# A causal attention layer and a two-layer shifted transformer on one core: stages joined early, whole rows copied one partition down, results stored from ScalarE's queue

## The reference

```
xn  = layernorm(x)
out = x + attn(xn) + ffn(xn)
# attn: 16 heads of 64, causal, relative position bias per head (a table over i-j), logits / 64,
#       softmax, @ v, heads joined @ Wo + bo
# ffn:  two layers, each
h = shift_token(x)                 # columns 64..127 come from the token before
q, k, v = split(h @ wqkv)          # 8 heads of 64
q = l2norm(q) * q_scale; k = l2norm(k) * k_scale; q, k = rotary_xpos(q, k)
x = x + local_attention(q, k, v) @ wo      # windows of 64, looking one window back
h = layernorm(shift_token(x)) * ln_g + ln_b
a, g = split(h @ w1 + b1)          # 341 columns each
x = x + (a * gelu(g)) @ w2 + b2
```

## Time and profile before

| | |
|---|---|
| time, 3 runs | 2707.05 us median (2701.14 to 6372.38) |
| profiled execution | 2707.02 us, its span 2705.2 us |
| TensorE matmul busy | 2547.8 us (94%), 24208 instructions |
| ScalarE / VectorE / GpSimd busy | 2158.3 (80%) / 2009.4 (74%) / 1629.7 us (60%) |
| mean granted TensorE clock | 0.977 of full speed |
| DMA packets | 128513, 77.07 MB |

### The profile page before, as it was taken

How to read it: one execution, slowest core, us unless ns; L and a number is a source line. 1 busy time by engine, 2 the same in 40 slices (tenths; PEclk the granted TensorE clock), 3 DMA queues, 4 the chain that set the end, 5 groups by cost and what they waited for, 6 DMA issues and landing times. The chain is left out here.

```text
span 2705.2 us, 71234 instructions
## 1 busy us (share of the span) xinstructions
PE 2547.8 (94%) x24208; PEld 1988.1 (73%) x24208; DVE 2009.4 (74%) x5647; ACT 2158.3 (80%) x6335; POOL 1629.7 (60%) x1947
## 2 busy tenths in 40 slices
PE   7999999999999999999599999997979999999796
PEld 4777777777777777777378888885767888888575
DVE  4666666666666666666389999995659999999565
ACT  5888888888888888888389999996438999999642
POOL 3444444444444444444389999994229999999521
PEclk8999999999999999999799999998989999999898
DMA  2000000000000000000311111111111111111112
GB/s 72 7 7 10 9 9 5 8 7 9 9 9 5 10 7 7 9 6 5 103 41 41 38 42 39 38 42 46 33 26 40 38 42 42 38 40 42 46 33 79
DMA packets 128513, 77.07 MB, mean 28 GB/s; under 512 B 80196, under 2 KB 110736, under 8 KB 128144
## 3 DMA queue, kind: packets, MB, share of 16 engines
q1 hardware_dynamic: 127968, 72.34, 10.9%
q10 hardware_dynamic: 176, 0.07, 0.0%
HBM read 17.58 MB, written 8.41 MB: 10 GB/s over the span
## 5 line engine op out<-in xcount | busy, mean ns | idle before, releaser
L306 POOL TENSOR_SCALAR L<-L,rinv 128x128 f32<-128x128 f32 (+3 forms) x1024 | 522.4, 533 | 622.7 <-DVE rinv L488 622.7
L370 ACT ACTIVATE L<-L,nmax 128x384 f32<-128x384 f32 (+3 forms) x1024 | 571.8, 561 | 144.2 <-DVE nmax L474 144.2
L474 DVE CUSTOM_DVE_ANT_0 L<-bank,bias_tab 128x256 f32<-128x256 f32 (+3 forms) x1024 | 470.5, 479 | 180.3 <-PE bank L590 178.3
L886 ACT ACTIVATE f_L<-bank,f_nmax,f_rn 128x128 f32<-128x128 f32 x1024 | 459.9, 486 | 5.0 <-DVE f_nmax L1013 5.0
L863 POOL TENSOR_TENSOR f_rn<-f_ssq,f_mhalf 128x16 f32<-128x16 f32 x128 | 419.1, 3274 | 18.2 <-DVE f_ssq L997 4.7
L845 POOL TENSOR_TENSOR f_qkr<-f_ab 128x256 f32<-128x256 f32 x512 | 414.3, 838 | 10.3 <-DVE f_ab L964 10.3
L611 PE MATMUL bank<-ident,L 128*128 128x128 f32 x2560 | 370.4, 276 | 2.3 <-DVE PT L215 2.0
L611 PEld LDWEIGHTS bank<-ident,L 128*128 128x128 f32 x2560 | 296.8, 141 | 83.4 <-issue 46.1
L964 DVE TENSOR_TENSOR f_ab<-bank,f_tab 128x512 f32<-128x512 f32 x512 | 347.8, 680 | 8.8 <-ACT f_sq L876 8.8
L632 PE MATMUL bank<-PT,v 128*64 128x512 f32 (+3 forms) x2048 | 303.9, 439 | 0.6 <-DVE yacc L507 0.4
L632 PEld LDWEIGHTS bank<-PT,v 128*64 128x64 f32 x2048 | 126.8, 136 | 166.2 <-issue 164.9
(11 more groups left out here) (145 smaller groups left out, 6390.8 us busy)
## 6 DMA issues: line engine op xcount, KB each, us to landing
f_vm<-f_v SPq DMA_DIRECT2D x224, 128.0 KB, 2.4
f_hs<-xf SPq DMA_DIRECT2D x132, 32.0 KB
f_hs<-xf SPq DMA_DIRECT2D x132, 31.8 KB
xb<-in_L_attn_x SPq DMA_DIRECT2D x16, 256.0 KB, 2.8
out<-yacc SPq DMA_DIRECT2D x32, 128.0 KB, 1.8
f_hs<-xf SPq DMA_DIRECT2D x32, 128.0 KB
out<-f_acc SPq DMA_DIRECT2D x4, 1024.0 KB, 7.5
f_hs<-xf SPq DMA_DIRECT2D x32, 127.0 KB
```

The source lines that it names most:

```text
L306: nc.gpsimd.tensor_scalar(t, t, rinv[:, h % RING, a, i:i + 1], 1.0, ALU.mult, ALU.mult).then_inc(s_N, 1)
L370: nc.scalar.activation(t, t, ACT.Exp, bias=nmax[:, ep % RING, a, i:i + 1], scale=-1.0, accum_out=rsum[:, ep % RING, a, i:i + 1]).then_inc( ...
L474: nc.vector.tensor_tensor_reduce(out=L[:, p % RING, a, LOFF[i]:LOFF[i] + (i + 1) * P], in0=ps_s[a][i], in1=bias_tab[:, 2 * p + a, T - (i + ...
L886: nc.scalar.activation(L[:, ot % 2, a, k, :], ps_s[a][:, k * P:k * P + P], ACT.Exp, bias=nmax[:, ot % 2, a, k:k + 1], scale=rn[:, ot % 2, ...
```

## The change

- **Layers unrolled.** The loop over the two layers is written out; addresses are constants.
- **Block between removed.** Its loads and masks go into the causal stage: GpSimd builds the masks in slot (0, 6), SP loads the first shifted tiles in batch 1 and layer 0's tables and weights in batch 15 into the bias table's space, GpSimd multiplies the tables and splits `wqkv` in the last three slots (`prepare_attention`, eight steps).
- **Attention to MLP.** Batch 0's statistics to low half, batch 1's statistics and the halves of `w1` go into attention's drain slots. The MLP's loads of batches 0 and 1 go into attention's batches 4 and 5.
- **MLP to attention.** Layer 0's MLP loads layer 1's tables and weights in slots 4 to 6, its first shifted tiles in slots 7 to 10, and prepares them on GpSimd in slots 7 to 14.
- **MLP rows.** Four buffers; batches 0 and 1 are copied as before, the others as below; ScalarE writes the unshifted half.
- **MLP order.** `hidden(0)`, `hidden(1)`, transposes, `second` in one run, `hidden(2)`; VectorE's second gating comes before the residual.
- **End.** `out` is read back in tile (6, 0) of layer 0's attention. In layer 1's MLP GpSimd adds `xf` to `acc` batch by batch, VectorE adds the product to `acc`, and ScalarE's queue stores each batch.
- **Causal slot 4.** On ScalarE `value_out` and `xT_high` stand before an exponential each, on VectorE `xT_low` before the addition to `yacc`.

The core of the diff:

```
@@ causal_attention, sync
+                if b == B - 1:
+                    sp.wait_ge(s_L, at(b, 8 * HP, 8 * 4))
+                    for part in range(3):
+                        load_attention_weights(sp, c, d, w, 0, part, w["s_load"])
+                if b == 1:
+                    sp.wait_ge(s_xf, 1)
+                    sp.wait_ge(w["s_hs_zero"], 1)
+                    for t in range(TT):
+                        load_shifted(sp, c["hs"], xf, 0, t, w["attn"][f"hs{t}"])
@@ causal_attention, gpsimd
+                if (b, p) == (0, 6):
+                    build_masks(nc, pool, c, w)
+                for n in {(B - 1, 6): (0, 1, 2), (B - 1, 7): (3, 4, 5), (B, 0): (6, 7)}.get((b, p), ()):
...
+                    prepare_attention(nc, pool, c, w, n, w["s_load"])
@@ causal_attention, scalar
+                if p == 4 and item is not None:
+                    value_out(item)
                 exps(2, 1)
-                if item is not None:
+                if p == 4 and has_scores(b) and has_next(b):
+                    xT_high(b + 1, 1 - par)
+                if p != 4 and item is not None:
                     value_out(item)
                 exps(0, 1)
@@ causal_attention, vector
                 logits(3, 0)
+                if p == 4 and has_scores(b) and has_next(b):
+                    xT_low(b + 1, 1 - par)
                 if step is not None:
@@ load_shifted_batch
-def load_shifted_batch(sp, hs, xf, b, r, s_hs):
+def load_shifted_batch(sp, w, xf, b):
+    hs, s_hs = w["shifted"][b % 4], w["mlp"][f"hs{b % 4}"]
+    if b < 2:
+        sp.dma_start(hs[:, :, 0:half], x_b[:, :, 0:half]).then_inc(s_hs, 16)
+        sp.dma_start(hs[1:P, :, half:D], x_b[0:P - 1, :, half:D]).then_inc(s_hs, 16)
+    else:
+        sp.dma_start(hs[1:P, :, :], x_b[0:P - 1, :, :]).then_inc(s_hs, 16)
+    sp.dma_start(hs[0:1, 1:TT, half:D], x_b[P - 1:P, 0:TT - 1, half:D]).then_inc(s_hs, 16)
+def batch_own_half(nc, act, w, xf, b):
+    act.wait_ge(w["mlp"][f"hs{b % 4}"], batch_rows_count(b))
+    nc.scalar.activation(w["shifted"][b % 4][:, :, 0:half], xf[:, b * TT:b * TT + TT, 0:half],
+                         ACT.Copy).then_inc(w["mlp"]["half"], 1)
@@ local_attention
+            if b in (4, 5) and t == 0:                                    # sync
+                sp.wait_ge(w["s_fill"], 4)
+                sp.wait_ge(sem["x_out"], 2 * TT)
+                load_shifted_batch(sp, w, xf, b - 4)
+            if (l, b, t) == (0, 6, 0):
+                sp.dma_start(w["acc"][:], d["out"].rearrange("b (t p) d -> p (b t) d", p=P)).then_inc(w["s_acc"], 16)
+            if (b, t) == (B, 1):                                          # gpsimd
+                batch_scale(nc, pool, w, 0)
+            if (b, t) == (B, 2):
...
+            if (b, t) == (B + 1, 0):
+                batch_low(nc, pool, w, 0)
+            if (b, t) == (B + 1, 0):                                      # scalar
+                batch_affine(nc, act, c, w, 0)
+            if (b, t) == (B, 0):                                          # vector
+                batch_statistics(nc, dve, w, 0)
+            if (b, t) == (B, 2):
+                batch_normalise(nc, dve, w, 0)
+                batch_statistics(nc, dve, w, 1)
+            if (b, t) == (B, 3):                                          # tensor
+                batch_transposes(nc, pe, c, w, 0)
@@ gated_mlp
-        load_attention_weights(sp, c, d, 1 - l, sem["weights"])
-            sp.wait_ge(sem["hn"], at(b, TT, -TT))
+            if 2 <= b < B:                                                # sync
+                sp.wait_ge(sem["hn"], at(b, TT, -3 * TT))
+                load_shifted_batch(sp, w, xf, b)
+            if nxt is not None and 4 <= b < 7:
+                load_attention_weights(sp, c, d, w, nxt, b - 4, sem["weights"])
+            if nxt is not None and 7 <= b < 11:
+                sp.wait_ge(sem["x_out"], 1)
+                load_shifted(sp, c["hs"], xf, 0, b - 7, w["attn"][f"hs{b - 7}"])
+            if l < DEPTH - 1 and 7 <= b < 15:                             # gpsimd
+                prepare_attention(nc, pool, c, w, b - 7, sem["weights"])
+            if l == DEPTH - 1 and now is not None:
+                pool.wait_ge(w["s_acc"], 16)
+                a = w["acc"][:, b * TT:b * TT + TT, :]
+                nc.gpsimd.tensor_tensor(a, a, xf[:, b * TT:b * TT + TT, :], ALU.add).then_inc(sem["acc"], 1)
+            if l == DEPTH - 1 and four is not None:                       # scalar
+                act.wait_ge(sem["x_out"], four + 1)
+                act.dma_start(d["out"]..., w["acc"][:, four * TT:four * TT + TT, :]).then_inc(w["s_stored"], 16)
+            if 2 <= b + 1 < B:
+                batch_own_half(nc, act, w, xf, b + 1)
@@ transformer
-        with nc.Fori(0, DEPTH) as l:
+        for l in range(DEPTH):
             local_attention(nc, c, d, l, w)
             gated_mlp(nc, c, d, l, w)
```

More of the change, by code:

```diff
@@ new lines, in batch_scale, with batch_transposes @@
+def batch_scale(nc, pool, w, b):
+    pool.wait_ge(w["mlp"]["ve"], b + 1)
+    nc.gpsimd.tensor_tensor(w["rstd"][:], w["ve"][:], w["mhalf"][:, 0:TT], ALU.pow).then_inc(w["mlp"]["rstd"], 1)
+def batch_transposes(nc, pe, c, w, b):
+    sem, ps_t = w["mlp"], c["bank"][6]
+    pe.wait_ge(sem["hn"], TT * (b + 1))
+    pe.wait_ge(sem["hT_hi"], b)
+    for t in range(TT):
+        last = nc.tensor.transpose(ps_t[:, t * P:t * P + P], w["hn"][:, t, :], c["ident"][:])
+    last.then_inc(sem["T_done"], 1)
@@ new lines, in batch_low, with batch_normalise @@
+def batch_low(nc, pool, w, b):
+    sem = w["mlp"]
+    pool.wait_ge(sem["hT_out"], b + 1)
+    pool.wait_ge(sem["hT_hi"], b + 1)
+    nc.gpsimd.tensor_tensor(w["mT_lo"][:, b % 2, :], w["mT"], w["mT_hi"][:, b % 2, :].bitcast(F32),
+                            ALU.subtract).then_inc(sem["hT_lo"], 1)
+def batch_normalise(nc, dve, w, b):
+    sem = w["mlp"]
+    dve.wait_ge(sem["rstd"], b + 1)
+    dve.wait_ge(sem["T_done"], b)
+    for t in range(TT):
+        nc.vector.tensor_scalar(w["hn"][:, t, :], w["shifted"][b % 4][:, t, :], w["mv"][:, t, 0:1], w["rstd"][:, t:t + 1],
+                                ALU.subtract, ALU.mult).then_inc(sem["hn"], 1)
@@ L1207, in _ @@
+            if now is not None and b > 0:
+                batch_scale(nc, pool, w, b)
+            if l < DEPTH - 1 and 7 <= b < 15:
[4 more added lines that the diff above has]
+                nc.gpsimd.tensor_tensor(a, a, xf[:, b * TT:b * TT + TT, :], ALU.add).then_inc(sem["acc"], 1)
         batch_slots(pool, slot, 3)
@@ L1295, in hidden, with second @@
                     nc.tensor.matmul(ps[0:n, :], w1_hi[:, col], hT_lo[:, r, :], start=False, stop=True).then_inc(sem["ga_done"], 1)
-            def second(tiles):
-                for t in tiles:
+            def second():
+                for t in range(TT):
                     for j in range(3):
@@ L1310, in slot @@
             hidden(0)
+            if two is not None:
+                pe.wait_ge(sem["H"], at(two, 3, -1))
+            hidden(1)
+            if one is not None and one > 0:
+                batch_transposes(nc, pe, c, w, one)
             if three is not None:
@@ L1313, in slot @@
                 pe.wait_ge(sem["x_out"], at(three, 1, 0))
-                second(range(2))
-            if one is not None:
-                pe.wait_ge(sem["hn"], at(one, TT, TT))
-                pe.wait_ge(sem["hT_hi"], at(one, 1, 0))
-                for t in range(TT):
-                    last = nc.tensor.transpose(ps_t[:, t * P:t * P + P], hn[:, t, :], ident[:])
-                last.then_inc(sem["T_done"], 1)
-            if three is not None:
-                second(range(2, TT)).then_inc(sem["y_done"], 1)
+                second()
             if two is not None:
                 pe.wait_ge(sem["H"], at(two, 3, 0))
-            hidden(1)
             hidden(2)
```

361 lines of the change are left out of this document (180 added, 181 removed).

## The result

The changed kernel takes **2776.94 us** (median; 2774.84 to 2778.23) against 2704.73 us: ratio 1.0267 [1.0255, 1.0279], 2.7% slower. 2725 us was predicted, with a range of 2668 to 2772; the time lies 5 us above the range. The profiled execution took 2775.99 us, with a span of 2773.8 us against 2705.2. One execution of the kernel before (6372.38 us, still in the median of four here) and one of experiment 8 (3542.03 us, left out of the time given there) ran far slower than the others and count in no ratio.

What follows compares the result with a forecast made beforehand. TensorE was taken to bound the causal stage, GpSimd attention, one DMA engine's 127-row copy the MLP. From 2707.0 us, +36.3 +32.9 -21 -7.5 -16.5 +2 -7.5 = +18.7 gave 2725.7, said as 2725 us; range 2668 to 2772.

Steps and rivals of the forecast that it cites:

- What bounds the MLP: MLP: the shifted 127-row copy on one DMA engine, 7.2 us of the 8.02 us period, sets the pace.
- Rival 1: MLP: the copy isn't the limit, TensorE sets the pace at 7.5 us a batch; 2624 us, chance 0.10.
- I take 10.1 us: MLP: time of the new copy of 127 rows of 2 KB on one engine, making the period 10.1 instead of 8.02 us.
- Rival 2: MLP: the one engine is slower on long rows, 12 us (2779 us) or 14.4 us (2846 us) a copy; chance 0.16.
- To this the layer's own traffic ... is added: MLP: other traffic on the same engine, 12 us in layer 0 (tables, weights, tiles), 8 us in layer 1 (stores).
- the drain's term: Attention to MLP, both layers: +2.7 us, of which 1.2 stand under attention and 1.5 under the MLP.
- The read-back: Attention of layer 0, tile 24: reading back 4 MB ahead of rows wanted about two tiles later costs 0 to 5 us, +2 taken.
- The drain: End of attention: 2.7 us of new VectorE work against a gap of 1.58 us makes it 1.2 us later.
- Joins and end: Causal stage to attention -21 us, MLP to attention -7.5 us, last residual to the end -16.5 us.
- the causal slot: Pair 4 of each causal batch: `xT_lo` moved ahead starts 0.56 us sooner, -7.5 us over 15 batches.
- Rival 3: Joins: they give little, through held-up drains or code fetch, with loads as forecast; 2745 us, chance 0.10.
- The new order of the MLP: MLP: would remove TensorE's wait of 0.5 us a batch, but is worth nothing under a load period of 10.1 us.

Runs made afterwards that it cites:

- experiment 8: Experiment 6 with the causal stage's old order in the slot of pair 4: 2636.61 us, ratio 0.9756.
- experiment 2: The changed kernel with its whole-row copy of 127 MLP rows cut into 112 and 15 rows: 2655.25 us, ratio 0.9817.
- experiment 4: The changed kernel with its whole-row copy of 127 MLP rows cut into 113 and 14 rows: 2745.88 us, ratio 1.0151.
- experiment 1: The changed kernel with MLP rows loaded as before in 256 B pieces, four buffers kept, ScalarE's half copy gone: 2700.29 us, ratio 0.9984.
- Experiment 6: The changed kernel with every 127-row copy cut into 112 and 15 rows and the read-back in sixteen pieces: 2628.88 us, ratio 0.9722.
- Experiment 5: The changed kernel with the 4 MB read-back of `out` cut into sixteen copies of 256 KB: 2763.15 us, ratio 1.0217.
- experiment 10: Experiment 6 with MLP rows in halves without ScalarE's copy, plus batch 0's normalising and batch 1's statistics one drain slot later: 2617.07 us, ratio 0.9674.
- experiment 9: The changed kernel with GpSimd's split of `w1` in attention's drain made to wait for VectorE's four normalising steps: 2776.43 us, ratio 1.0272.
- experiment 11: Experiment 10 with batch 0's statistics and their power also one slot later: 2613.44 us, ratio 0.9659.
- experiment 3: The kernel before with only its one-row-down copy cut into 112 and 15 rows: 2683.43 us, ratio 0.9920.

## Why the prediction was wrong

**What bounds the MLP: right.** One engine carries the shifted copy; experiments 2 and 4 change only how it is cut, experiment 1 its bytes (and ScalarE's copy with them), and the times come within 6, 1 and 8 us of their forecasts. Rival 1 (the copy isn't the limit) falls by the same runs.

**"I take 10.1 us": right.** 10.2 us measured, 80 ns a piece. Taken with the 14.2 ns of a 256 B piece, that gives 27.1 GB/s for the bytes and 4.8 ns for the piece itself, an estimate from two sizes. The 28.4 GB/s that served as a bound was read too high: the half microsecond of the earlier trace rows has a DMA share of 1.13, so more was counted in it than it can hold. Rival 2 (12 or 14.4 us) falls; that the time ended near its 2779 us is chance.

**"To this the layer's own traffic ... is added", 12 and 8 us: mis-sized.** From the first issue of the loads to the last residual pass 189.0 us in layer 0. Less the 24.1 us of tail and 14 x 10.2 us, 22 us are left, not 12; 17.8 of them lie between the loads of batches 4 and 12 (99.4 us for eight), where weights and tiles are sent. In layer 1 the same sum, 179.0 - 24.1 - 14 x 10.2, leaves 12 us for the stores, 0.9 us for each of 14 loads, where I had counted 8. With 1.3 us more for the block's start this makes the 11.3 and 5.2 us by which the MLPs exceed their terms (14 x 0.1 us for the period and the 1.5 us that the drain's term had put here cancel). How layer 0's 22 us divide between weights, tiles and SP's held issues isn't settled; in experiment 2 all of it but 0.5 us is gone.

**The loads of MLP batches 0 and 1 within attention: a term that was missing.** I had priced their absence in the MLP and not their presence in attention: two copies a layer, of 7.2 us each, on the very engine that attention's tile rows need, in a stage in which GpSimd has no gap. They cost 7.7 us in layer 0 and 6.6 us in layer 1 of this execution; in layer 0 of experiment 2, with the same code in attention, the same four tiles cost 11.6 us. Experiment 6 takes them away with the cut.

**The read-back, "0 to 5 us, I take +2": wrong.** 12.0 us. "Rows wanted about two tiles later" was the fault. The copy of 4 MB takes 17.5 us and stands ahead of the next tiles' rows: GpSimd's power for such a tile came 9.7 us late, so those rows had about one tile's time of slack, not two (17.5 - 9.7 us). The rest of the 12.0 us is in the tile after it, 10.1 us long, in which the granted clock was 0.50 (1516 to 1526 us). Experiment 5 gives 13.8 us back.

**The drain, "1.2 us later": wrong.** From the even half's reciprocal to the last residual it is 4.3 us in layer 0 and 5.5 in layer 1. I had set VectorE's 2.7 us of new work against an idle 1.58 us by its duration in the MLP, where GpSimd was idle at that moment. In the drain GpSimd works beside it, and VectorE is held: 3.71 us for 1.10, and the odd half's product starts 3.5 us later. The rest, 0.8 and 2.0 us, lies behind that product, on TensorE's path: from the product to the last residual 8.3 us pass in both layers at a granted clock that fell to 0.50 for 6.8 us within TensorE's wait of 4.2 us for the product, against 7.5 us in layer 0 before (0.50 for 3.4 us) and 6.2 in layer 1 before (1.00 throughout); in experiment 10 it is 6.2 us again. No run changes the clock alone, so its share is argued. Another 1.2 us a layer came from the statistics one slot earlier, ahead of the last tile's sums, a step that I hadn't priced. Experiments 9 to 11 show both steps.

With that, attention's two sums close. Layer 0: 7.7 (loads) + 12.0 (read-back) + 1.2 (statistics) + 1.2 (the other tiles, 7.85 us for 7.83) + 4.0 (last power to last residual) = 26.1 us, 25.9 measured. Layer 1: 6.6 + 1.2 + 1.2 + 6.8 and 0.9 for a longer tile at its start, 16.7 us as measured.

**Joins and end: right**, -46.8 us against -45. So is the causal slot: -9.3 us by experiment 8, -7.5 forecast. I had read TensorE's wait for `xT_lo` from the matmul's row (0.68 us) and not from its weight load's, which waited 15.5 us in 16 batches and now waits 6.6. Rival 3 (the joins give little) falls.

**The new order of the MLP, worth nothing under the loads: right**, and it gives nothing between batches with the loads spread either: both orders take 7.29 us. The wait that it was to remove came from the loads, and was 0.7 us, read as 0.5 from one of two rows (experiment 3).

In sum, the direction was right. Of the 50 us missed 38 lie in attention and 16.5 in the MLPs, and 5 came back in the joins and the causal stage. The work moved into attention was priced where it had come from, not where it went.

## What to carry to other kernels

A copy shifted by one partition has 127 rows, and lands on one DMA engine; cut at 112 rows it left the pace of every stage here. See first how many engines a copy uses (a steady DMA share of 0.06), before its bytes are moved to another engine or its pieces made longer. When work is moved into a busy stage, price it by who shares its queue and its port there: the same 130 KB and the same four instructions were hidden in one place and cost 3 to 4 us each time in another. Where TensorE waits, read the row of its weight load together with the matmul's: twice here the gain lay nearer to the weight load's wait.

## What the runs showed of the hardware

- One DMA engine moves 256 B pieces at 18 GB/s and 2 KB pieces at 25 GB/s. The Trainium skill ("DMA: Bandwidth & Descriptors", section "Where 436 GB/s comes from") has 435.2 GB/s for the ports that a core's sixteen engines share, by estimate 27 GB/s an engine; the trace stays a little under it.
- VectorE's `tensor_scalar` from SBUF to SBUF was held while GpSimd ran: up to 1.78 us for one step of 0.33 us, and 1.25 us for one of 0.17 us. Its `bn_stats` wasn't (0.86 us for four, with GpSimd beside them and without). The Trainium skill ("SBUF — State Buffer", section "SBUF: two separate sides") tells of a port pair of the two engines that one of them locks for a whole instruction; these rows agree: the held step of 0.17 us ended with GpSimd's instruction.
- With one large copy on a single engine under way, SP's queue takes the next one and holds the issue behind it: the small copy of row 0 shows 9.5 to 10.2 us where it takes 0.7 us at the start of the MLP. So a long row of an issue can belong to the copies ahead of it.
- In the changed kernel's MLP of layer 0 TensorE's granted clock was 0.87 on the mean, and 0.50 (the level of 1.2 GHz) in 1990 to 1992 us, after waits of up to 9.9 us of TensorE for `batch_low`. With the loads spread it was 1.00. The loads set the pace there, so the lower clock cost nothing that shows; in attention's drain it stood on the path: eight matmuls of the output product took 1.91 us at 0.50 and 1.06 us at 1.00.
